# Three norm groups closed with 65 columns, gamma applied by VectorE, and a new order of closings and rounds

## The chip, the cores and the metric

The kernel runs on one core of one Trainium2 chip. The metric is the device time of one execution in microseconds (us), lower is better. TensorE is the matrix engine, VectorE, ScalarE and GpSimd the others that compute; SyncE issues most transfers. A profile names them PE, DVE, ACT, POOL and SP; PEld is TensorE's loading of weights.

## The reference, cut to what matters

```python
def layer0(ego, adj, W_u, diag_u, par_u, W_i, diag_i, par_i, ln_gamma, ln_beta):
    u = par_u[0] * par_u[1] * (diag_u[:, None] * ego[:2048] @ W_u) + ego[:2048]
    i = par_i[0] * par_i[1] * (diag_i[:, None] * ego[2048:] @ W_i) + ego[2048:]
    e = jnp.concatenate([u, i], axis=0)                 # 5120 x 64
    h = adj @ (adj.T @ e)                               # adj 5120 x 5120, float32
    mu, var = jnp.mean(h, -1, keepdims=True), jnp.var(h, -1, keepdims=True)
    return (h - mu) * rsqrt(var + 1e-5) * ln_gamma + ln_beta + ego

x = layernorm(x + layer0(x, adj, ...))
x = layernorm(x + layer1(x, adj, ...))    # graph message passing; zero where no edge survives
```

The second layer's messages are zero if no edge can pass its thresholds. The kernel proves that for its inputs by a bound on the sums of squares of `adj`'s pieces (the maximum below) and takes the long way only if the proof fails. With these inputs it does not take it.

## The kernel before, in words

`adj` passes through the chip once. It is cut into ten blocks of 512 columns, and a block into twenty units of two 128-row tiles. For each unit TensorE multiplies rows of e by it (`multiply_unit`, L1471, which sums adj.T @ e of the block), ScalarE squares and sums it for the maximum, and VectorE transposes it in place. Once a block's sums are complete, its share of h, transposed (64 features by row tiles), is made in rounds (`multiply_round`, L1491), each over some of the forty row tiles: the last block has the rounds LAST (tiles 0 to 11), LAST + 1 (12 to 23), LATE + 1 (24 to 31) and LATE + 2 (32 to 39), and LATE is the last round of the block before, over sixteen tiles (24 to 39). A round's sums lie in four banks of PSUM, and VectorE adds them to `h_sum` (`add_tiles`, L1285), which raises `round_added`. All of LAST + 1 to LATE + 2 use the same banks, so each waits for the addition of the one before.

`h_sum` then is turned to rows and normed in seven groups, `NORM_PARTS`: group k is tiles first to first + nt, sizes 6, 6, 4, 8, 8, 4, 4. To close a group (`close_tiles`, L1506) means one matmul for each tile, with the tile's 128 x 128 piece of `h_sum` as weights and `center` as the moving operand. `center` has 128 columns: 64 give the features less their mean, 64 the same times gamma. `center` is float32, and each such matmul appears in a profile as two passes, two loads and two products. The rest of a group is a chain over engines: ScalarE squares (`square_c`, L1183), VectorE sums (`sum_c`, L1337), GpSimd takes the root (`root_c`, L1107), VectorE scales and adds x (`make_y`, L1357 and L1364, or L1347), ScalarE squares again (`square_y`, L1191), VectorE sums (`sum_y`, L1369), GpSimd takes the second root (`root_y`, L1112), VectorE or ScalarE makes the output (`make_out`), and SyncE stores it.

Each engine works in the order in which its calls are written. `max_found` counts the steps of the maximum: VectorE's partial maximum, TensorE's product that brings it to one row (L1560), VectorE's reduction. Each engine reads the resulting flag once (`edges_may_survive`).

```python
                first, nt = NORM_PARTS[k]
                pe.wait_ge(round_added, added_through(k))
                if k == 1:
                    pe.wait_ge(max_found, 3)
                if k >= 2:
                    pe.wait_ge(t_made, k - 1)
```

Closing 4 is of tiles 24 to 31, so it needs the additions of LATE and LATE + 1; closings 5 and 6 need the two halves of the addition of LATE + 2.

## Time and profile before

| | |
|---|---|
| time, median of 3 runs | 395.99 us (395.52 to 396.37) |
| time of the profiled execution | 397.39 us |
| its span, first to last instruction | 395.5 us |
| TensorE busy | 379.0 us |
| VectorE busy | 316.7 us |
| ScalarE busy | 269.1 us |
| GpSimd busy | 63.8 us |

The span is what the profile shows; starting and ending the program lie around it. Matmuls are pipelined, so a busy TensorE need not be at its peak. Work moves the time only where it lies on the chain that ended last.

### The profile page before, as it was taken

The numbers are of one execution on the slowest core, as the hardware profiler recorded it, in microseconds if no ns is written. First come the engines' busy times: TensorE is split into PE (matmuls) and PEld (weight loads), VectorE is DVE, ScalarE is ACT, GpSimd is POOL, SyncE is SP. The second block draws the span as 40 slices with busy tenths as digits, with TensorE's granted clock in tenths as the row PEclk, the third lists the DMA queues.
The fourth block names the chain that finished last, engine by engine and source line by source line (L and its number), as shares of the span: only waits on it lengthen the run. The fifth ranks groups of instructions, "written<-read, shape, count | busy, mean of one in ns | idle before, by whom it ended". The sixth has DMA issues, their size and how long they took to land.

```text
span 395.5 us, 13309 instructions
## 1 busy us (share of the span) xinstructions
PE 379.0 (96%) x5762; PEld 220.2 (56%) x5762; DVE 316.7 (80%) x305; ACT 269.1 (68%) x519; POOL 63.8 (16%) x122
## 2 busy tenths in 40 slices
PE   8987999999999999999999999999999999999990
PEld 7743655565465546545654664565466456555770
DVE  1699989797697869687976989697698869795674
ACT  3598996994868658597856868685876778511143
POOL 2001101102100300030030003003000300277375
PEclk9999999999999999999999999999999999999996
DMA  8999999995797799579877958996795799400012
GB/s 291 387 388 382 386 386 384 386 352 192 232 380 267 268 320 391 180 275 389 314 263 272 386 195 277 388 351 230 278 386 191 272 392 383 145 3 2 24 35 85
DMA packets 56991, 109.83 MB, mean 278 GB/s; under 512 B 3808, under 2 KB 4576, under 8 KB 56928
## 3 DMA queue, kind: packets, MB, share of 16 engines
q1 hardware_dynamic: 56640, 108.84, 76.3%
q8 instruction: 47, 0.77, 0.8%
q14 instruction: 16, 0.13, 0.1%
q10 hardware_dynamic: 288, 0.09, 0.1%
HBM read 107.60 MB, written 1.31 MB: 275 GB/s over the span
## 4 chain that ended last, share of the span: by engine, by line
PE 84%; DMA 6%; issue 3%; DVE 3%; POOL 1%; ACT 1%; SPq 1%; POOLq 0%; DVEq 0%
PE quad L1491 45%; PE quad L1471 34%; DMA pooled<-in_adj 6%; PE quad L1506 2%; DVE pooled L1265 2%; PE quad L1513 1%; PE quad L1442 1%; ACT scratch L1153 1%; SPq L1033 1%; PE quad L1452 1%; DVE pooled L1285 1%; POOL pooled L1112 1%; POOL col_sum L1084 0%; POOLq L96 0%; POOL pooled L1107 0%
## 5 line engine op out<-in xcount | busy, mean ns | idle before, releaser
L1153 ACT ACTIVATE scratch<-pooled 128x1024 bf16<-128x1024 f32 x200 | 210.1, 1051 | 39.8 <-DMA pooled<-in_adj 38.0
L1265 DVE STREAM_TRANSPOSE pooled<-pooled 128x1024 f32<-128x1024 f32 x200 | 229.7, 1209 | 3.3 <-ACT scratch L1153 3.2
L1471 PE MATMUL quad<-pooled,rows_in 128*64 128x256 f32 x1600 | 180.2, 381 | 4.3 <-DMA pooled<-in_adj 4.3
L1491 PE MATMUL quad<-pooled,col_sum 32*64 32x320 f32 (+4 forms) x3968 | 177.5, 507 | 0.4 <-POOL col_sum L1084 0.2
L1471 PEld LDWEIGHTS quad<-pooled,rows_in 128*64 128x64 f32 x1600 | 111.9, 137 | 74.3 <-issue 13.1
L1491 PEld LDWEIGHTS quad<-pooled,col_sum 32*64 32x64 f32 x3968 | 87.5, 132 | 83.1 <-issue 64.6
L1285 DVE TENSOR_TENSOR pooled<-pooled,quad 128x1280 f32<-128x1280 f32 (+5 forms) x29 | 52.4, 1808 | 43.8 <-PE quad L1491 43.7
L1084 POOL COPY col_sum<-col_half 32x256 f32<-32x256 f32 x80 | 31.6, 394 | 312.1 <-DVE col_half L1274 309.0
L1162 ACT COPY col_sum<-col_half 32x256 f32<-32x256 f32 x80 | 32.2, 402 | 38.0 <-DVE col_half L1274 37.0
L1153 ACT ACTIVATION_READ_ACCUMULATOR scratch<-pooled 128x1 f32 x200 | 37.4, 187 | 0.0
L1183 ACT ACTIVATE pooled<-quad 128x256 f32<-128x256 f32 (+2 forms) x7 | 3.3, 475 | 23.4 <-PE quad L1506 23.4
L1506 PEld LDWEIGHTS quad<-center,pooled 128*128 128x128 f32 x80 | 9.3, 191 | 3.3 <-issue 1.8
L1506 PE MATMUL quad<-center,pooled 128*128 128x128 f32 x80 | 10.3, 281 | 0.9 <-DVE pooled L1285 0.8
L1274 DVE STREAM_TRANSPOSE col_half<-quad 128x256 f32<-128x256 f32 x10 | 4.5, 445 | 7.2 <-PE quad L1471 7.2
L1112 POOL TENSOR_TENSOR pooled<-pooled,minus_half 128x4 f32<-128x4 f32 (+2 forms) x7 | 8.9, 1276 | 6.5 <-DVE pooled L1369 6.4
L1107 POOL TENSOR_TENSOR pooled<-pooled,minus_half 128x4 f32<-128x4 f32 (+2 forms) x7 | 8.9, 1281 | 5.0 <-DVE pooled L1337 4.8
L1191 ACT ACTIVATE pooled<-pooled 128x256 f32<-128x256 f32 (+2 forms) x7 | 3.6, 507 | 9.1 <-DVE pooled L1364 7.2
L1147 ACT COPY pooled<-quad 128x512 f32<-128x512 f32 x5 | 2.9, 585 | 9.7 <-PE quad L1442 9.7
L1283 DVE COPY pooled<-quad 128x1280 f32<-128x1280 f32 (+2 forms) x3 | 5.8, 1936 | 4.1 <-PE quad L1491 4.1
L1238 DVE TENSOR_TENSOR rows_in<-quad,pooled 128x256 f32<-128x256 f32 x10 | 3.7, 410 | 3.6 <-PE quad L1452 3.3
L1102 POOL TENSOR_TENSOR pooled<-pooled,beta_sb 128x512 f32<-128x512 f32 x5 | 6.4, 1276 | 0.4
L1337 DVE TENSOR_REDUCE pooled<-pooled 128x4 f32<-128x260 f32 (+2 forms) x7 | 3.8, 538 | 2.7 <-ACT pooled L1183 2.7
(45 smaller groups left out, 62.8 us busy)
## 6 DMA issues: line engine op xcount, KB each, us to landing
pooled<-in_adj SPq DMA_DIRECT2D x200, 512.0 KB, 9.4
pooled<-in_x SPq DMA_DIRECT2D x5, 256.0 KB, 3.7
pooled<-in_x SPq DMA_DIRECT2D x1, 768.0 KB, 5.3
pooled<-in_x SPq DMA_DIRECT2D x1, 512.0 KB, 3.8
out<-pooled SPq DMA_DIRECT2D x2, 256.0 KB, 2.5
out<-pooled SPq DMA_DIRECT2D x2, 192.0 KB, 2.4
out<-pooled SPq DMA_DIRECT2D x3, 128.0 KB, 2.1
pooled<-in_w_ui ACTq DMA_DIRECT2D x1, 64.0 KB, 3.3
```

Source lines behind the costliest of these rows:

```text
L1084: kept = nc.gpsimd.tensor_copy(spread_to(c, a, h, 1), spread_from(c, h, 1))
L1102: nc.gpsimd.tensor_tensor(xk, xk, beta_sb[:, :].unsqueeze(1).to_broadcast([P, GT, D]), ALU.add).then_inc(x_steps, 1)
L1107: nc.gpsimd.tensor_tensor(rstd[:, norm_tiles(k)], var[:, norm_tiles(k)], minus_half[:, 0:norm_size(k)], ALU.pow).then_inc(rstd_made, 1)
L1112: nc.gpsimd.tensor_tensor(scale[:, norm_tiles(k)], y_var[:, norm_tiles(k)], minus_half[:, 0:norm_size(k)], ALU.pow).then_inc(scale_made, 1)
L1153: nc.scalar.activation(scratch[v % 2][:, :], slots[slot_of(v)], ACT.Square, accum_out=square_sum[:, v:v + 1]).then_inc(unit_scanned, 1)
L1162: kept = act.copy(spread_to(c, a, h, 0), spread_from(c, h, 0))
L1265: nc.vector.transpose(tiles, tiles).then_inc(unit_turned, 1)
L1283: nc.vector.tensor_copy(to, share).then_inc(round_added, 1)
L1285: nc.vector.tensor_tensor(to, to, share, ALU.add).then_inc(round_added, 1)
L1471: mm = pe.matmul(block_bank(c)[half(h), 0:w // 2], rows_in[:, t, :], slots[slot_of(v)][:, at:at + w // 2], start=(t == 0), stop=(t == T - 1))
L1491: mm = pe.matmul(round_banks(g)[a][half(b % 2), 0:w].rearrange("p (t r) -> p t r", r=32), col_sum[c % 2][quadrant(a), b, :], to[quadrant(a ...
L1506: mm = pe.matmul(nat_of(k)[:, i, :], h_sum[:, P * (first + i):P * (first + i) + P], center[:, :], start=True, stop=True)
```

## The change

The first three groups (`NARROW = 3`) are closed with 65 columns of a `center` of 129: 64 centred features and one column with each row's share of gamma's mean. VectorE makes the product with gamma from those, with `gamma_row`, a copy of gamma in all partitions, by two operations a group (`take_c`). The maximum's product moves ahead of the closings, closings 0 and 1 both ahead of round LATE, and 2 and 3 ahead of LATE + 1. The sequences of VectorE, ScalarE and GpSimd are rewritten to suit; groups 0 and 1 exchange the engines that make their output.

```diff
-    BY_ACT, BY_DVE = (1, 2, 3), (0, 4, 5, 6)
+    BY_ACT, BY_DVE = (0, 2, 3), (1, 4, 5, 6)
+    NARROW = 3
-        ln_t = [ln_buffer(D) for _ in range(2)]
+        ln_t = [ln_buffer(D) for _ in range(3)]
-        center = sb("center", [P, 2 * D])
+        center = sb("center", [P, 2 * D + 1])
+        gamma_row = sb("gamma_row", [P, D])
-            return bank[(4 if upper_banks(LAST) else 0) + 3]
+            return bank[(4 if upper_banks(LAST) else 0) + 1][:, CH - P:CH]
...
+                    sp.dma_start(gamma_row[:, :], gamma.rearrange("d o -> (d o)").partition_broadcast(P)).then_inc(norm_in, 16)
...
-                    act.copy(center[:, D:2 * D], bank[3][:, 0:D]).then_inc(center_kept, 1)
+                    act.copy(center[:, 0:D], bank[3][:, 0:D]).then_inc(center_kept, 1)
+                    act.copy(center[:, 2 * D:2 * D + 1], bank[3][:, D:D + 1]).then_inc(center_kept, 1)
...
+                nc.vector.tensor_scalar(center_g[:, D:D + 1], gamma_sb[:, :], 0.5 / D, None, ALU.mult).then_inc(gamma_made, 1)
+                nc.vector.tensor_scalar(gamma_row[:, :], gamma_row[:, :], 0.5, None, ALU.mult).then_inc(gamma_steps, 1)
...
+            def take_c(k):
+
+                nt = norm_size(k)
+                dve.wait_ge(c_squared, k + 1)
+                if k == 0:
+                    dve.wait_ge(gamma_steps, 1)
+                nc.vector.tensor_tensor(ln_t[k][:, 0:nt, :], features_of(k),
+                                        gamma_row[:, :].unsqueeze(1).to_broadcast([P, nt, D]), ALU.mult).then_inc(c_scaled, 1)
+                dve.wait_ge(c_scaled, k + 1)
+                nc.vector.tensor_tensor(ln_t[k][:, 0:nt, :], ln_t[k][:, 0:nt, :],
+                                        nat_of(k)[:, 0:nt, D:D + 1].to_broadcast([P, nt, D]),
+                                        ALU.subtract).then_inc(nat_taken, 1)
...
-                if k == 1:
+                if k >= 2 + NARROW:
+                    pe.wait_ge(t_made, k - 1)
+                elif k >= 2:
+                    pe.wait_ge(nat_taken, k - 1)
+                if k == 2:
                     pe.wait_ge(max_found, 3)
-                if k >= 2:
-                    pe.wait_ge(t_made, k - 1)
+                kinds = slice(D, 2 * D + 1) if k < NARROW else slice(0, 2 * D)
                 for i in range(nt):
-                    mm = pe.matmul(nat_of(k)[:, i, :], h_sum[:, P * (first + i):P * (first + i) + P], center[:, :],
+                    mm = pe.matmul(nat_of(k)[:, i, 0:kinds.stop - kinds.start],
+                                   h_sum[:, P * (first + i):P * (first + i) + P], center[:, kinds],
                                    start=True, stop=True)
...
             multiply_round(LAST)
             multiply_round(LAST + 1)
+            pe.wait_ge(max_found, 1)
+            pe.wait_ge(round_added, added_through(0))
+            pe.matmul(max_bank()[0:1, :], part_max[:, :], ident[:, :], start=True, stop=True).then_inc(max_found, 1)
             close_tiles(0)
-            pe.wait_ge(max_found, 1)
-            pe.matmul(max_bank()[0:1, 0:P], part_max[:, :], ident[:, :], start=True, stop=True).then_inc(max_found, 1)
+            close_tiles(1)
             multiply_round(LATE)
-            close_tiles(1)
             close_tiles(2)
+            close_tiles(3)
             multiply_round(LATE + 1)
-            close_tiles(3)
             close_tiles(4)
             multiply_round(LATE + 2)
```

TensorE before, from round LAST on (L1491 a round, of 64 products; L1506 closings, L1560 the maximum's product):

```order
L1491 MATMUL quad<-pooled,col_sum 64x384 x128
L1506 MATMUL quad<-center,pooled 128x128 x6
L1560 MATMUL quad<-ident,part_max 1x128
L1491 MATMUL quad<-pooled,col_sum 64x512 x64
L1506 MATMUL quad<-center,pooled 128x128 x10
L1491 MATMUL quad<-pooled,col_sum 64x256 x64
L1506 MATMUL quad<-center,pooled 128x128 x16
L1491 MATMUL quad<-pooled,col_sum 64x256 x64
L1506 MATMUL quad<-center,pooled 128x128 x8
```

TensorE with the change, the same stretch (L1526 a round, L1545 closings, L1600 the maximum's product):

```order
L1526 MATMUL quad<-pooled,col_sum 64x384 x128
L1600 MATMUL quad<-ident,part_max 1x128
L1545 MATMUL quad<-center,pooled 128x65 x12
L1526 MATMUL quad<-pooled,col_sum 64x512 x64
L1545 MATMUL quad<-center,pooled 128x65 x4
L1545 MATMUL quad<-center,pooled 128x128 x8
L1526 MATMUL quad<-pooled,col_sum 64x256 x64
L1545 MATMUL quad<-center,pooled 128x128 x8
L1526 MATMUL quad<-pooled,col_sum 64x256 x64
L1545 MATMUL quad<-center,pooled 128x128 x8
```

Twelve tiles in place of six are closed ahead of round LATE, twelve in place of ten ahead of LATE + 1, and eight in place of sixteen ahead of LATE + 2.

VectorE before, between round LAST + 1's addition and LATE's (L1337 sum_c, L1397 and L1399 the maximum and flag, L1357 and L1364 make_y, L1369 sum_y, L1377 make_out, L1285 the addition):

```order
L1337 TENSOR_REDUCE pooled<-pooled 128x6
L1397 TENSOR_REDUCE all_max<-quad 1x1
L1399 TENSOR_SCALAR flag<-all_max 1x1
L1357 TENSOR_TENSOR pooled<-quad,pooled 128x384
L1364 TENSOR_TENSOR pooled<-pooled 128x384
L1369 TENSOR_REDUCE pooled<-pooled 128x6
L459 TENSOR_LOAD flag
L459 ISA x2
L1377 TENSOR_TENSOR pooled<-pooled 128x384
L1285 TENSOR_TENSOR pooled<-pooled,quad 128x4x16x32
```

VectorE with the change, the same stretch up to the read of the flag (L1353 sum_c, L1362 and L1365 take_c, L1432 and L1434 maximum and flag, L1389 and L1396 make_y); the addition follows it:

```order
L1353 TENSOR_REDUCE pooled<-pooled 128x6
L1362 TENSOR_TENSOR pooled<-quad,gamma_row 128x384
L1365 TENSOR_TENSOR pooled<-pooled,quad 128x384
L1353 TENSOR_REDUCE pooled<-pooled 128x6
L1362 TENSOR_TENSOR pooled<-quad,gamma_row 128x384
L1365 TENSOR_TENSOR pooled<-pooled,quad 128x384
L1432 TENSOR_REDUCE all_max<-quad 1x1
L1434 TENSOR_SCALAR flag<-all_max 1x1
L1389 TENSOR_TENSOR pooled<-pooled 128x384
L1396 TENSOR_TENSOR pooled<-pooled 128x384
L1389 TENSOR_TENSOR pooled<-pooled 128x384
L1396 TENSOR_TENSOR pooled<-pooled 128x384
```

Group 1's first half stands there now, with the two operations of take_c for both groups, while group 0's last sum moves behind the addition and its output to ScalarE.

VectorE before, at the last two additions (4x4x32):

```order
L1357 TENSOR_TENSOR pooled<-quad,pooled 128x512
L1285 TENSOR_TENSOR pooled<-pooled,quad 128x4x4x32
L1369 TENSOR_REDUCE pooled<-pooled 128x8
L1285 TENSOR_TENSOR pooled<-pooled,quad 128x4x4x32
L1364 TENSOR_TENSOR pooled<-pooled 128x512
```

VectorE with the change, there (L1401 sum_y, L1409 make_out, L1301 the additions):

```order
L1401 TENSOR_REDUCE pooled<-pooled 128x8
L1409 TENSOR_TENSOR pooled<-pooled 128x384
L1389 TENSOR_TENSOR pooled<-quad,pooled 128x512
L1301 TENSOR_TENSOR pooled<-pooled,quad 128x4x4x32 x2
L1396 TENSOR_TENSOR pooled<-pooled 128x512
```

The sum for group 3 now stands ahead of both additions, and the output of group 1 with it.

## Rows read from the trace of the kernel before

**Rows 1.** The page: engines, GB/s by slice, chain by engine.

```profile
PE 379.0 (96%) x5762; PEld 220.2 (56%) x5762; DVE 316.7 (80%) x305; ACT 269.1 (68%) x519; POOL 63.8 (16%) x122
...
GB/s 291 387 388 382 386 386 384 386 352 192 232 380 267 268 320 391 180 275 389 314 263 272 386 195 277 388 351 230 278 386 191 272 392 383 145 3 2 24 35 85
...
PE 84%; DMA 6%; issue 3%; DVE 3%; POOL 1%; ACT 1%; SPq 1%; POOLq 0%; DVEq 0%
```

**Rows 2.** Timeline, PE, from 359 us: start, length (us), line, count.

```profile
359.72 1.60 PE L1506 MATMUL quad<-center,pooled 128*128 128x128 f32 x12
361.25 0.38 PE L1560 MATMUL quad<-ident,part_max 128*1 128x128 f32 x2
361.79 7.13 PE L1491 MATMUL quad<-pooled,col_sum 32*64 32x512 f32 x128 [0.16 <-DVE pooled L1285]
368.85 2.50 PE L1506 MATMUL quad<-center,pooled 128*128 128x128 f32 x20
371.45 3.71 PE L1491 MATMUL quad<-pooled,col_sum 32*64 32x256 f32 x128
375.09 3.84 PE L1506 MATMUL quad<-center,pooled 128*128 128x128 f32 x32
378.86 3.71 PE L1491 MATMUL quad<-pooled,col_sum 32*64 32x256 f32 x128
383.42 2.36 PE L1506 MATMUL quad<-center,pooled 128*128 128x128 f32 x16 [0.85 <-DVE pooled L1285]
```

**Rows 3.** Timeline, DVE, from 359 us; columns as above.

```profile
359.89 1.75 DVE L1285 TENSOR_TENSOR pooled<-pooled,quad 128x1536 f32<-128x1536 f32 x1 [2.01 <-PE quad L1491]
361.95 0.56 DVE L1337 TENSOR_REDUCE pooled<-pooled 128x6 f32<-128x390 f32 x1 [0.30 <-ACT pooled L1183]
...
364.12 0.56 DVE L1357 TENSOR_TENSOR pooled<-quad,pooled 128x384 f32<-128x384 f32 x1 [1.25 <-POOL pooled L1107]
...
369.01 2.29 DVE L1285 TENSOR_TENSOR pooled<-pooled,quad 128x2048 f32<-128x2048 f32 x1 [0.59 <-PE quad L1491]
...
375.25 1.22 DVE L1285 TENSOR_TENSOR pooled<-pooled,quad 128x1024 f32<-128x1024 f32 x1
...
382.04 0.69 DVE L1357 TENSOR_TENSOR pooled<-quad,pooled 128x512 f32<-128x512 f32 x1 [0.30 <-POOL pooled L1107]
382.68 0.69 DVE L1285 TENSOR_TENSOR pooled<-pooled,quad 128x512 f32<-128x512 f32 x1
...
383.88 0.68 DVE L1285 TENSOR_TENSOR pooled<-pooled,quad 128x512 f32<-128x512 f32 x1
```

**Rows 4.** The chain that ended last, in order of time: start, length, what.

```profile
384.62 1.17 PE quad L1506 x8
...
386.73 1.01 POOL pooled L1107
```

**Rows 5.** Timeline, PEld: loads of weights (rows*columns, then shape).

```profile
9.08 0.97 PEld L1452 LDWEIGHTS quad<-pooled 64*128 64x128 f32 x16 [0.17 <-issue]
...
368.85 2.31 PEld L1506 LDWEIGHTS quad<-center,pooled 128*128 128x128 f32 x20 [0.81 <-issue]
...
383.42 0.97 PEld L1506 LDWEIGHTS quad<-center,pooled 128*128 128x128 f32 x8 [1.30 <-DVE pooled L1285]
```

**Rows 6.** Timeline, ACT and POOL, behind closing 4.

```profile
378.97 0.60 ACT L1183 ACTIVATE pooled<-quad 128x512 f32<-128x512 f32 x1 [1.19 <-PE quad L1506]
...
380.37 1.64 POOL L1107 TENSOR_TENSOR pooled<-pooled,minus_half 128x8 f32<-128x8 f32 x1
```

**Rows 7.** Early: timelines of PE and DVE, PE's waits 40 to 360, issues.

```profile
39.90 4.57 PE L1491 MATMUL quad<-pooled,col_sum 32*64 32x320 f32 x128 [0.16 <-POOL col_sum L1084]
...
56.97 2.02 DVE L1283 COPY pooled<-quad 128x1792 f32<-128x1792 f32 x1 [1.12 <-PE quad L1491]
...
PE quad L1471 <- DMA pooled<-in_adj: 0.7, 3, 0.3
...
beta_sb<-in_beta SPq DMA_DIRECT2D x1, 32.0 KB, 9.7
```

More of the change, by code:

```diff
@@ L66, in adjacency_layers_kernel @@
     NORMS = len(NORM_PARTS)
-    BY_ACT, BY_DVE = (1, 2, 3), (0, 4, 5, 6)
+    BY_ACT, BY_DVE = (0, 2, 3), (1, 4, 5, 6)
+    STORES = (0, 1, 2, 4, 5, 3, 6)
     SHORT = 5
+    NARROW = 3
     BOUND = 0.2
@@ L255, in adjacency_layers_kernel @@
         rstd_made = sem("rstd_made")
+        gamma_steps = sem("gamma_steps")
+        c_scaled = sem("c_scaled")
+        nat_taken = sem("nat_taken")
         t_made = sem("t_made")
@@ L396, in max_bank, with features_of @@
         def max_bank():
-            return bank[(4 if upper_banks(LAST) else 0) + 3]
+            return bank[(4 if upper_banks(LAST) else 0) + 1][:, CH - P:CH]
+        def features_of(k):
+            at = 0 if k < NARROW else D
+            return nat_of(k)[:, 0:norm_size(k), at:at + D]
         def round_sums(g, first, nt):
@@ L1047, in store_made @@
                 store_out(sp, k)
-            for k in (0, 1, 2, 4, 5, 3, 6):
+            for k in STORES:
                 store_made(k)
@@ L1065, in _ @@
                     pool.wait_ge(center_made, 1)
-                nc.gpsimd.affine_select(out=center[:, 0:D], in_=center[:, 0:D], compare_op=ALU.not_equal, fill=1.0,
+                nc.gpsimd.affine_select(out=center[:, D:2 * D], in_=center[:, D:2 * D], compare_op=ALU.not_equal, fill=1.0,
                                         base=-D * h, pattern=[[-1, D]],
@@ L1069, in _ @@
             pool.wait_ge(center_made, 2)
-            nc.gpsimd.tensor_scalar(center[:, 0:D], center[:, 0:D], -1.0 / D, None, ALU.add).then_inc(center_made, 1)
+            nc.gpsimd.tensor_scalar(center[:, D:2 * D], center[:, D:2 * D], -1.0 / D, None, ALU.add).then_inc(center_made, 1)
             pool.wait_ge(ident_made, 1)
@@ L1122, in _ @@
             root_c(0)
+            root_c(1)
+            survives = edges_may_survive(pool)
             root_y(0)
-            survives = edges_may_survive(pool)
-            root_c(1)
             root_c(2)
+            root_c(3)
             root_y(1)
-            root_c(3)
+            root_y(2)
             root_c(4)
-            root_y(2)
             root_y(3)
@@ L1182, in square_c @@
                     act.wait_ge(var_made, k - 1)
[L1183 removed]
+                nc.scalar.activation(c_sq[k % 2][:, 0:norm_size(k), 0:D], features_of(k),
                                      ACT.Square, scale=D ** -0.5).then_inc(c_squared, 1)
@@ L1201, in _ @@
             square_c(0)
+            square_c(1)
+            survives = edges_may_survive(act)
             square_y(0)
-            survives = edges_may_survive(act)
-            square_c(1)
+            square_y(1)
             square_c(2)
-            square_y(1)
+            square_c(3)
+            make_out(0)
             square_y(2)
-            square_c(3)
             square_c(4)
-            make_out(1)
             square_y(3)
@@ L1356, in scale_y @@
                 dve.wait_ge(rstd_made, k + 1)
-                nc.vector.tensor_tensor(ln_t[k % 2][:, 0:nt, :], nat_of(k)[:, 0:nt, D:2 * D],
+                if k < NARROW:
+                    dve.wait_ge(nat_taken, k + 1)
+                source = ln_t[k] if k < NARROW else nat_of(k)
+                nc.vector.tensor_tensor(ln_t[k % 3][:, 0:nt, :], source[:, 0:nt, 0:D],
                                         over_row(rstd[:, tiles], nt), ALU.mult).then_inc(t_made, 1)
@@ L1363, in add_x @@
                 dve.wait_ge(x_steps, 1 + 2 * -(-tiles.stop // GT))
-                nc.vector.tensor_tensor(x_all[:, tiles, :], x_all[:, tiles, :], ln_t[k % 2][:, 0:nt, :],
+                nc.vector.tensor_tensor(x_all[:, tiles, :], x_all[:, tiles, :], ln_t[k % 3][:, 0:nt, :],
                                         ALU.add).then_inc(y_made, 1)
@@ L1395, in _ @@
             sum_c(0)
+            take_c(0)
+            sum_c(1)
+            take_c(1)
             dve.wait_ge(max_found, 2)
-            nc.vector.tensor_reduce(all_max[0:1, :], max_bank()[0:1, 0:P], X, ALU.max).then_inc(max_found, 1)
+            nc.vector.tensor_reduce(all_max[0:1, :], max_bank()[0:1, :], X, ALU.max).then_inc(max_found, 1)
             dve.wait_ge(max_found, 3)
@@ L1400, in _ @@
             make_y(0)
+            make_y(1)
+            survives = edges_may_survive(dve)
+            add_round(LATE)
             sum_y(0)
-            survives = edges_may_survive(dve)
-            make_out(0)
-            add_round(LATE)
-            sum_c(1)
             sum_c(2)
-            make_y(1)
+            sum_c(3)
+            sum_y(1)
+            take_c(2)
+            add_round(LATE + 1)
             make_y(2)
-            add_round(LATE + 1)
-            sum_y(1)
+            make_y(3)
             sum_y(2)
-            sum_c(3)
             sum_c(4)
-            make_y(3)
+            sum_y(3)
+            make_out(1)
             scale_y(4)
             add_tiles(NR - 1, *NORM_PARTS[NORMS - 2])
-            sum_y(3)
             add_tiles(NR - 1, *NORM_PARTS[NORMS - 1])
@@ L1481, in multiply_round @@
                 if g == before_in_banks(NR, False)[0]:
-                    pe.wait_ge(center_kept, 1)
+                    pe.wait_ge(center_kept, 2)
                 same = before_in_banks(g, upper_banks(g))
@@ L1537, in _ @@
             multiply_round(1)
-            pe.wait_ge(gamma_made, 1)
-            pe.matmul(bank[3][:, 0:D], center_t[:, :], center_g[:, :], start=True, stop=True).then_inc(gamma_turned, 1)
+            pe.wait_ge(gamma_made, 2)
+            pe.matmul(bank[3][:, 0:D + 1], center_t[:, :], center_g[:, :], start=True, stop=True).then_inc(gamma_turned, 1)
             for v in range(UNIT_FIRST[1] + 9, UNIT_FIRST[2]):
```

9 lines of the change are left out of this document (4 added, 5 removed).

## The prediction

> **What bounds the kernel now.** I read the page first. TensorE is busy 96% of the span and holds 84% of the chain that ended last [rows 1]. So a change at the end of the program is worth what it does to TensorE's sequence there. The timeline of TensorE from 359 us on shows that sequence: blocks of closings (L1506) and of rounds (L1491), each starting 0.07 us before the printed end of the one ahead, except where a row names a wait [rows 2]. The reader is to see three things in it. At 361.79 the round of sixteen tiles waited 0.16 us for VectorE's addition of round LAST + 1. At 371.45 the next round started 0.15 us after VectorE's addition of 2.29 us had ended at 371.30 [rows 3]: twenty passes of closings just covered it. At 378.86 nothing waited: sixteen tiles were closed after round LATE + 1, and the first eight of them (3.84 us for both, so 1.9) hid the addition of 1.22 us that began at 375.25 and that the second eight need. The chain of waits shows the end: closing 6 at 384.62, then, by way of a square and a sum, GpSimd's last roots from 386.73 on [rows 4]. A closing of one tile is two of the profile's passes.
>
> **What a narrow pass costs.** This decides the case. With 65 columns in place of 128 TensorE streams half as much, but it still loads the same 128 x 128 weights for each tile (a piece of h_sum). The trace has no closing of 65 columns; it has the product at L1452 with 64 moving columns and 128-column weights, sixteen passes that alternate between two halves of the rows, so eight for each half. Their loads fill 0.97 us. The eight loads of a closing of four tiles, which move 128 columns, fill 0.97 us as well [rows 5]. Less the 0.19 us that one load lasts (2.31 us for twenty gives (2.31 - 0.19)/19 = 0.112 us), the period of a load into the same rows is 0.111 to 0.112 us whether 64 or 128 columns follow. I take this as the bound: the load, not the stream, sets a closing's pace, and a narrow pass costs 0.112 us, as a wide one does. The other end: a pass costs what it streams, 65/128 of 0.112, thus 0.057 us. Taken together L1452's sixteen loads come every 0.052 us, but only because those into different halves of the rows overlap, which loads into all 128 rows can't. I stay near the upper end.
>
> The Trainium skill, "TensorE: Matmul & The Clock Gate", section "Back-to-back issue gap", gives an isolated matmul N/2.4 + 2.5 ns, thus 55.8 ns at 128 columns and 29.6 at 65; the trace shows twice the former for a float32 pass, so my estimate by the page is 0.059 us for a narrow pass, and the sum would then be that of the first rival below. The page adds that in a stream the loads count too; L1452 bears that out here.
>
> **The sequence on TensorE, step by step** (times of the profiled run, starts from [rows 2]; p is the narrow pass, 0.112).
> 1. The maximum's product comes first, at 359.72 in place of 361.25. It lasts 0.38 us, 0.31 until the next block: closings start at 360.03. Before, it lay where TensorE would have waited for the addition anyway.
> 2. Closings 0 and 1 are 24 passes. Twenty printed 2.50 us, so 24 make 2.95, and 2.88 until the next block: 362.91. The addition (359.89 + 1.75 = 361.64 [rows 3]) is long done. Before, the round started at 361.79: 1.12 us later.
> 3. Round LATE takes 7.06 us from start to start (361.79 to 368.85): 369.97. Its addition begins 0.16 later and ends at 372.42.
> 4. Closings 2 and 3, 8 narrow and 16 wide passes: 2.88 us, 372.85, past the addition. Before 371.45: 1.40 later.
> 5. Round LATE + 1: 3.64 us (371.45 to 375.09): 376.49. Now closing 4 stands directly behind it and needs h_sum as VectorE's addition leaves it. Before it began 0.16 after 375.09 and took 1.22, and TensorE resumes 0.05 after an addition (that at 382.68 ended 383.37, closing at 383.42). So TensorE idles until 376.49 + 0.16 + 1.22 + 0.05 = 377.92, 1.43 us.
> 6. Closing 4 is 16 passes: 2.50 - 4 x 0.112 = 2.05, 1.98 to the next block: 379.90. Round LATE + 2 follows. Before 378.86: 1.04 later. With starts of loads in place of starts of products I get 1.09.
> 7. The tail. VectorE does the sum for group 3 before round LATE + 2 ends, no longer between the last two additions. Before, the additions began at 382.68 and 383.88, and closing 6 waited for the second, which ended 384.56. Now the second follows 0.60 after the first. Closing 5's eight passes then allow closing 6 at 383.42 + 8 x 0.112 = 384.31 in old times, against 384.62: 0.31 us back. GpSimd's roots for group 3 also move out of the way of the last ones, so from closing 6 on the chain [rows 4] goes as it went.
> Sum: 1.04 to 1.09 less 0.31, that is 0.73 to 0.78 us later.
>
> **The rest of the change.** The scaling by gamma puts six operations on VectorE: four over 128 x 384 at about 0.56 us (as the broadcast product at 364.12, [rows 3]) and two of a third less. Ahead of LATE's addition it has two sums, four such operations, four of make_y and 0.4 us of maximum and flag: 10 x 0.56 + 0.4 = 6.0 us. The first sum starts 0.63 us after closing 0 ended (361.32 to 361.95), now 362.26, so VectorE is ready at 368.3, and the round ends at 369.97: 1.7 us spare. Ahead of LATE + 1's addition, the sum for group 3 can start at 372.92 + 0.63 = 373.5 and 2.1 us of work follow: 375.6 against 376.65. Both additions keep their time, so I cost this at nothing; the cover is those 1.7 and 1.0 us. The way from closing 4 to the addition of tiles 32 to 35 is a second lane beside round LATE + 2: square at 378.97, sum, root at 380.37 with 1.64 us [rows 6], product at 382.04, addition at 382.68 [rows 3]. It moves with closing 4, no further: root_y(2), ahead of it on GpSimd, has its sum about a microsecond earlier. What make_out(0) loses in time on ScalarE only delays a store that nothing waits for.
>
> Early in the program: a third small load on SP's queue beside beta's 32 KB, in a stretch where transfers set TensorE's pace up to about 39 us. Beta's load landed 9.7 us after its issue because of what stood ahead in the queue [rows 7]. Priced by bytes at the 388 GB/s of the page's early slices [rows 1], 32 KB are 0.08 us; round 0 at 39.90 waited for something else, so it costs 0 to 0.1. Two tiny VectorE operations near 46 us (0.15 to 0.3 us each) lie ahead of VectorE's idle time of 1.12 us at 56.97 [rows 7]; one more ScalarE copy of one column has no reader for a long while; from 40 to 360 us TensorE waited only 0.7 us for transfers [rows 7]. I add 0.05 at most. The profiled execution took 397.39 us with a span of 395.5; the median of the runs is 395.99, and I put the difference on that: 395.99 + 0.8 = **396.8 us**. What a measurement here can tell from no change is 0.2%, 0.79 us, so the forecast stands on that line, at 396.78.
>
> **Rivals.**
> - *The stream sets the pace* (p = 0.057). Then closings 0 and 1 end at 361.6, before the addition, and LATE starts at 361.79 as before. Closings 2 and 3 take 2.88 - 8 x 0.055 = 2.44 us, less than the 2.60 from 368.85 to 371.45, so the addition still sets that start. Behind LATE + 1, 1.43 idle and 1.98 for closing 4 stand in place of 3.77: 0.36 us sooner. With 0.31 in the tail it is 0.67 us, 395.3. For it: half the columns. Against it: the loads of L1452. The sum falls by 32 x (0.112 - p), so the sign changes at p = 0.088. Chance 0.10.
> - *VectorE comes late.* If the operations with gamma took twice 0.56 us, LATE's addition would start 4 x 0.56 - 1.7 = 0.5 us late. Closings 2 and 3 give it 2.88 us where it needs 2.60, so 0.2 us reaches LATE + 1. There another 2 x 0.42 us and the 0.5 stand against 1.0 us of margin, so 0.3 us more is added to the idle time: 397.3. For it: no row shows an operation with gamma. Against it: the two margins. Chance 0.10.
> - *In between*: a load of weights follows a shorter stream somewhat sooner, p = 0.100 (0.38 us less), or the tail gives back more: 396.3 to 396.5. Chance 0.12.
> - The forecast, 396.5 to 397.1: 0.68.
>
> **Numbers.** The forecast case lies about the line at 396.78, a little more above it, since both ways of counting and the early costs lead up to 0.83: 0.38 above, 0.30 below. Slower: 0.38 and the late case's 0.10, 0.48. Same: 0.30, 0.12 of the case in between, and half of the stream case, whose 395.3 is just short of 0.2% (395.2): 0.47. Faster: the other half, 0.05. The range, 395.8 to 397.5, leaves out the stream case and the far end of the late one.
>
> **What would show it.** In the changed profile: 24 passes of 128 x 65 in one row of about 2.95 us (1.6 would prove the rival); no wait at the sixteen-tile round; an idle time of about 1.4 us ahead of closing 4, ended by VectorE; closing 6 directly behind closing 5; span near 396.3. A wait ahead of LATE + 1, or one ahead of closing 2 for nat_taken, would make it wrong on the slow side.

## The result, and the profile after

The changed kernel takes 400.38 us (median of 4 runs, 399.14 to 400.85), the kernel before 395.89 in the same measurement. The ratio is 1.0099, with an interval of 1.0083 to 1.0116. The prediction was 396.8, at most 397.5, so it fails. The profiled execution took 400.20 us with a span of 398.0.

The page of the changed kernel: TensorE's busy time, its granted clock by slice, and GB/s by slice.

```profile
PE 379.2 (95%) x5762; PEld 219.2 (55%) x5762; DVE 319.3 (80%) x313; ACT 269.6 (68%) x520; POOL 63.7 (16%) x122
...
PEclk9999899999999999999999999999999999999997
...
GB/s 292 387 387 350 386 387 386 342 390 101 274 391 313 239 301 387 194 272 392 337 250 270 383 197 275 392 355 227 271 386 197 270 392 375 143 3 2 4 54 85
```

TensorE does the same work in the same busy time. Each figure of the last two rows stands for a slice of 10 us. In two places the page differs early on, where the prediction expected nothing: the fourth slice (30 to 40 us) moves 350 GB/s where it moved 382 [rows 1], and the fifth has a clock digit of 8. The timeline of TensorE shows the place. First the kernel before, around units 20 and 21 (L1471); round 0 follows at 39.90 [rows 7]:

```profile
37.33 1.08 PE L1471 MATMUL quad<-pooled,rows_in 128*64 128x256 f32 x8 [0.40 <-DMA pooled<-in_adj]
38.66 1.08 PE L1471 MATMUL quad<-pooled,rows_in 128*64 128x256 f32 x8 [0.25 <-DMA pooled<-in_adj]
...
44.40 5.83 PE L1471 MATMUL quad<-pooled,rows_in 128*64 128x256 f32 x52
```

The same view of the changed kernel:

```profile
39.15 1.08 PE L1506 MATMUL quad<-pooled,rows_in 128*64 128x256 f32 x8 [2.93 <-DMA pooled<-in_adj]
40.49 1.59 PE L1506 MATMUL quad<-pooled,rows_in 128*64 128x256 f32 x8 [0.26 <-DMA pooled<-in_adj]
42.01 5.67 PE L1526 MATMUL quad<-pooled,col_sum 32*64 32x320 f32 x128
47.62 2.59 PE L1506 MATMUL quad<-pooled,rows_in 128*64 128x256 f32 x22
```

TensorE waits 2.93 us for unit 20's part of the adjacency, where it waited 0.40. It is 1.82 us late there, 2.11 at round 0 (42.01 against 39.90), and 3.22 behind round 0 (47.62 against 44.40), because the same 128 products take 5.67 us in place of 4.57. Windows of the changed kernel over that stretch show why (the clock is the third column from the right):

```profile
36.00:39.10 3.10, 0.22 (x3) 0.00 (x0) 3.10 (x5) 1.51 (x5) 0.95 (x3) 1.00 1.00 384
39.10:40.90 1.80, 1.49 (x12) 0.82 (x14) 1.80 (x2) 1.73 (x6) 1.62 (x5) 1.00 1.06 401
40.90:44.40 3.50, 3.50 (x48) 1.59 (x51) 2.77 (x3) 3.48 (x7) 0.58 (x2) 0.51 1.05 387
44.40:47.60 3.20, 3.20 (x104) 1.57 (x88) 0.00 (x0) 3.20 (x9) 0.00 (x0) 1.00 1.07 389
```

After 3.10 us in which TensorE worked for 0.22, the granted clock was 1.00 for another 1.80 us, then 0.51 (the 1.2 GHz level) for 3.50 us, and 1.00 again (2.4 GHz). At the lower level the same products take longer: 0.51 us more in unit 21 (1.59 against 1.08) and 1.10 in round 0.

Of these 3.22 us the two profiles keep 1.82 when the tail begins (361.54 against 359.72). The other 1.4 are the profile of before's own. It waited for transfers again, at two places, where the changed one waited for none from 48 to 360 us:

```profile
122.43 1.08 PE L1471 MATMUL quad<-pooled,rows_in 128*64 128x256 f32 x8 [0.27 <-DMA pooled<-in_adj]
...
157.08 1.08 PE L1471 MATMUL quad<-pooled,rows_in 128*64 128x256 f32 x8 [0.17 <-DMA pooled<-in_adj]
158.45 1.08 PE L1471 MATMUL quad<-pooled,rows_in 128*64 128x256 f32 x8 [0.29 <-DMA pooled<-in_adj]
```

This is also by how much its 397.39 us lay above its median. The trace of rows_load_alone (below) has neither of these waits, and a span of 394.3 us. Then the tail on TensorE, changed kernel (where a row joins passes of two shapes, it prints the first: the second row of x24 is 8 narrow and 16 wide passes):

```profile
361.54 0.38 PE L1600 MATMUL quad<-ident,part_max 128*1 128x128 f32 x2
361.85 2.89 PE L1545 MATMUL quad<-center,pooled 128*128 128x65 f32 x24
364.67 7.12 PE L1526 MATMUL quad<-pooled,col_sum 32*64 32x512 f32 x128
371.72 2.94 PE L1545 MATMUL quad<-center,pooled 128*128 128x65 f32 x24
374.60 3.71 PE L1526 MATMUL quad<-pooled,col_sum 32*64 32x256 f32 x128
379.69 2.05 PE L1545 MATMUL quad<-center,pooled 128*128 128x128 f32 x16 [1.38 <-DVE pooled L1301]
381.67 3.71 PE L1526 MATMUL quad<-pooled,col_sum 32*64 32x256 f32 x128
386.23 2.05 PE L1545 MATMUL quad<-center,pooled 128*128 128x128 f32 x16 [0.85 <-DVE pooled L1301]
```

From the start of the first of these blocks to the end of the last it is 26.74 us; before it was 385.78 - 359.72 = 26.06 [rows 2]. So the tail gives away 0.68 us, where the prediction had 0.73 to 0.78.

**Where the time went.** Early 3.2 us, tail 0.7. A third piece lies outside the span: time less span is 2.19 us on average in the changed kernel's runs, and 1.81 to 1.86 in those of the kernel before, some 0.35 more. The sum, 4.2 to 4.3, stands against a measured 0.0099 x 395.9 = 3.9 (3.3 to 4.6).

### The profile page after: what moved, and what is told of

It reads as the page before. It is cut to its first block, busy times and chain, and to the rows that moved or that the text cites. A ratio compares the mean times of both kernels' runs of the same rounds, so it can differ in the third digit from the quotient of the medians.

```text
span 398.0 us, 13320 instructions
## 1 busy us (share of the span) xinstructions
PE 379.2 (95%) x5762; PEld 219.2 (55%) x5762; DVE 319.3 (80%) x313; ACT 269.6 (68%) x520; POOL 63.7 (16%) x122
## 4 chain that ended last, share of the span: by engine, by line
PE 87%; SPq 7%; DMA 3%; POOL 1%; DVE 1%; issue 0%; POOLq 0%; ACT 0%
PE quad L1526 45%; PE quad L1506 40%; SPq L1046 5%; DMA pooled<-in_adj 3%; PE quad L1545 2%; SPq L1036 1%; POOL pooled L1125 1%; SPq L1031 1%; POOL pooled L1120 0%; DVE pooled L1301 0%; POOLq L98 0%; SPq L1037 0%; DVE pooled L1353 0%; SPq L1038 0%; DVE pooled L1409 0%
## 5 line engine op out<-in xcount | busy, mean ns | idle before, releaser
L1506 PE MATMUL quad<-pooled,rows_in 128*64 128x256 f32 x1600 | 180.1, 382 | 5.4 <-DMA pooled<-in_adj 5.4
L1526 PE MATMUL quad<-pooled,col_sum 32*64 32x320 f32 (+4 forms) x3968 | 178.6, 510 | 0.0
L1506 PEld LDWEIGHTS quad<-pooled,rows_in 128*64 128x64 f32 x1600 | 112.3, 137 | 74.4 <-issue 12.5
L1526 PEld LDWEIGHTS quad<-pooled,col_sum 32*64 32x64 f32 x3968 | 86.3, 133 | 85.0 <-issue 64.1
L1301 DVE TENSOR_TENSOR pooled<-pooled,quad 128x1280 f32<-128x1280 f32 (+5 forms) x29 | 52.3, 1808 | 45.1 <-PE quad L1526 45.1
L1545 PE MATMUL quad<-center,pooled 128*128 128x128 f32 (+1 forms) x80 | 9.9, 279 | 2.2 <-DVE pooled L1301 2.2
L1545 PEld LDWEIGHTS quad<-center,pooled 128*128 128x128 f32 x80 | 9.2, 192 | 4.2 <-DVE pooled L1301 3.1
L1553 PE MATMUL quad<-pooled 128*128 128x256 f32 x10 | 4.6, 650 | 1.2 <-DVE pooled L1238 1.2
```

What stands on the lines that cost most here:

```text
L1301: nc.vector.tensor_tensor(to, to, share, ALU.add).then_inc(round_added, 1)
L1506: mm = pe.matmul(block_bank(c)[half(h), 0:w // 2], rows_in[:, t, :], slots[slot_of(v)][:, at:at + w // 2], start=(t == 0), stop=(t == T - 1))
L1526: mm = pe.matmul(round_banks(g)[a][half(b % 2), 0:w].rearrange("p (t r) -> p t r", r=32), col_sum[c % 2][quadrant(a), b, :], to[quadrant(a ...
L1545: mm = pe.matmul(nat_of(k)[:, i, 0:kinds.stop - kinds.start], h_sum[:, P * (first + i):P * (first + i) + P], center[:, kinds], start=True, ...
```

## The experiments

Each kernel's ratio is to runs of the kernel before on the same chip; 95% intervals in brackets.

### The third small load, by itself and with other contents

gamma_load_alone is the kernel before with the one load added (and VectorE's wait for it):

```
+ sp.dma_start(gamma_row[:, :], gamma.rearrange("d o -> (d o)").partition_broadcast(P)).then_inc(norm_in, 16)
```

> The kernel before, with nothing of the change but the third small load (gamma to all 128 partitions, 256 bytes each) behind beta's, and VectorE waiting for it. Theory A (this load makes some of the transfer engines fall behind, so the parts of the next units land 1 to 2 us later, TensorE idles ahead of unit 20 and its clock drops for a while): the profile shows an idle time of 1.5 us or more ahead of the products at about 37 us, and the time is 1.5 to 4 us over the kernel before. Theory B (the early delay comes from something else in the change, as the reordered tail or the larger center, or is chance): within 0.3 us of the kernel before.

399.71 us, ratio 1.0094 [1.0077, 1.0111], thus 3.7 us: nearly the whole loss. TensorE's timeline:

```profile
39.62 3.33 PE L1473 MATMUL quad<-pooled,rows_in 128*64 128x256 f32 x16 [2.87 <-DMA pooled<-in_adj]
42.88 4.94 PE L1493 MATMUL quad<-pooled,col_sum 32*64 32x320 f32 x128
```

rows_load_alone reads x[0:P, :] instead: the same 32 KB in the same 128 pieces of 256 bytes, but from 128 different places.

> As the run with the gamma load alone, but the load brings 128 different rows of x, 256 bytes each, into the same tile, which nothing reads. Theory A1 (all 128 pieces read the same 256 bytes of HBM, and that is what is slow): no delay, within 0.3 us of the kernel before. Theory A2 (128 short pieces in the queue are what is slow, wherever they read): the same 1.5 to 4 us as with the gamma load.

396.44 us, ratio 1.0002 [0.9991, 1.0013]. It costs nothing that can be measured. So neither the bytes nor the short pieces are the cause; what is left is that one stretch of 256 bytes is read 128 times. gamma_load_twice has the load of gamma's row two times:

> The kernel before with the load of gamma to all partitions added twice, into two tiles, where the run with the gamma load alone has it once (3.3 us of early loss there). If each such load holds back the engines that it meets by about as much again: 6 us or more in all, with the last part of unit 20 landing near 42 us in place of 39.6. If it was one engine's mishap: as with one load, 3 to 4 us.

401.18 us, ratio 1.0122 [1.0104, 1.014], an idle time of 4.59 us ahead of unit 20, whose products start at 41.03. That is 4.8 us in the timed runs and 5.7 in the trace (50.11 behind round 0, against 44.40), short of the 6 expected and more than the 3 to 4 of the other theory. The view of the transfers shows what happens: GB/s from 30 to 42 us, in 40 slices of 0.3 us. The kernel before:

```profile
GB/s 382 382 375 396 396 382 389 375 396 357 342 360 369 375 389 369 410 376 382 376 410 382 369 396 389 375 403 369 403 382 389 375 389 376 396 396 403 369 382 375
```

The changed kernel, with the row above it, the busy share of the DMA engines in tenths (9 is 90% or more):

```profile
DMA  9999999999975866678989999999999999999999
GB/s 382 369 382 369 396 396 382 396 369 367 319 220 219 262 237 237 235 287 322 378 349 349 384 373 379 389 403 416 389 410 396 416 382 389 410 403 369 403 396 369
```

rows_load_alone:

```profile
GB/s 369 376 396 369 382 416 376 389 376 344 350 329 370 362 382 365 380 375 403 369 423 355 382 382 389 389 382 403 376 396 382 382 389 382 382 396 396 355 396 389
```

gamma_load_twice:

```profile
GB/s 376 376 376 382 355 403 382 396 382 351 303 206 151 177 172 179 146 172 173 198 187 225 191 205 230 277 382 362 329 313 361 343 335 362 423 403 423 382 403 396
```

From 33.3 us on, while gamma's row is under way (issued at 27.09, landed at 37.7), everything that the queue carries goes at 220 to 290 GB/s for about two microseconds; with two such loads it is below 230 for four. In the trough the engines are busy only 5 to 8 tenths of a slice; the kernel before has a 9 in each of the 40. So they stand idle between packets.

Unit 20's adjacency, which stands next in the queue, lands late, and not as a whole. The trace records sixteen landings for each transfer. In the changed kernel the first five of unit 20 come at 34.96 to 35.12 us, as in the kernel before (34.94 to 35.10), the other eleven at 35.51 to 39.10, where before they came at 35.12 to 37.28. TensorE needs all sixteen, so the slowest sets its start: from 30 to 42 us 4.29 MB were moved in place of 4.59, which at 383 GB/s is 0.8 us, but the last part was 1.8 us late.

gamma_rows_from_host is the changed kernel, with 128 copies of gamma's row laid out in memory beforehand:

```
- sp.dma_start(gamma_row[:, :], gamma.rearrange("d o -> (d o)").partition_broadcast(P)).then_inc(norm_in, 16)
+ sp.dma_start(gamma_row[:, :], gamma_rows).then_inc(norm_in, 16)
```

> The changed kernel as it is, all three small loads in their place ahead of unit 20, but the third reads 128 copies of gamma that lie one behind the other in HBM (an input laid out so) in place of 128 times the same 256 bytes. Theory A1 (reading the same 256 bytes 128 times holds the engines back): the early loss is gone, the last part of unit 20 lands by 37.5 us, 0.1% to 0.4% over the kernel before. Theory A2 (short pieces, wherever they read): 399 to 401 as the changed kernel.

397.28 us, ratio 1.0021 [1.0006, 1.0037]; the longest early wait is 0.51 us and round 0 starts at 40.23. What is left is what the rest of the change costs. No version with the changed tail has a lower ratio (the intervals of the next ones overlap with it), and it doesn't beat the kernel before.

### Why the load of beta's row did not cost as much

In the kernel before, beta's load copies one row to all partitions as well. beta_row_twice loads beta's row a second time in place of gamma's. beta_from_rows loads gamma's row as gamma_load_alone does, but beta from 128 rows.

```
beta_row_twice:  sp.dma_start(gamma_row[:, :], beta.partition_broadcast(P)).then_inc(norm_in, 16)
beta_from_rows:  sp.dma_start(beta_sb[:, :], beta_rows).then_inc(norm_in, 16)
```

> The kernel before with one more load of 32 KB in the place of the third small load, which copies the row of beta to all 128 partitions, as the load ahead of it already does. Theory A, two loads that each read one stretch of 256 bytes 128 times within a microsecond or two hold the transfers back together: as with gamma's row, about 3.2 us later, ratio 1.008 to 1.010, an idle time of some 2.9 us ahead of unit 20, and a trough near 220 GB/s between 33 and 36 us. Theory B, it is gamma's 256 bytes that are slow to read (the load of single elements ahead of it reads them as well): no loss, within 0.2% of the kernel before, 380 GB/s.

> The kernel before with gamma's row copied to all partitions as in the changed kernel, but beta's load reads 128 rows laid out one behind another, so that only one load of the program reads a stretch of 256 bytes 128 times. Theory A, one such load is nearly free, as beta's is in the kernel before, and the loss comes with the second: within 0.2% of the kernel before and 350 GB/s or more between 33 and 36 us. Theory B, gamma's row is slow by itself: about 3.2 us later, ratio 1.008 to 1.010.

399.3 us, ratio 1.0084 [1.0063, 1.0105], and 396.52 us, ratio 1.0014 [0.9995, 1.0033]. GB/s from 30 to 42 us in beta_row_twice:

```profile
GB/s 423 369 362 369 403 382 369 410 396 345 348 289 278 253 232 218 232 252 274 321 303 357 375 369 362 343 409 410 403 376 416 403 403 376 423 416 362 396 376 376
```

And in beta_from_rows:

```profile
GB/s 430 348 382 369 396 382 376 396 396 359 319 355 335 381 375 388 372 387 362 410 376 376 396 382 403 376 396 382 382 396 376 403 382 389 376 396 389 376 382 382
```

It is not gamma's row: with one copied row the stream stays at 319 GB/s or more, whichever row it is, and the second one directly behind it brings the trough. (Each of these ratios is to a kernel that itself has one copied row; no run is without any.) That is why the trace of before held no warning in beta's load. Why two of them do so, in the memory or in the transfer engines, stays open.

### The loads moved back in time

after_loads_later issues all three small loads behind units 20 and 21 (at v == UNIT_FIRST[1] + 2), before_loads_later does so with the two of the kernel before.

> The changed kernel with its three small loads (gamma, beta, gamma to all partitions) issued behind units 20 and 21 of adj in place of ahead of them. TensorE needs unit 22 only about 4 us after unit 21, since round 0 lies between. Theory A (the loads' place in the queue causes the early loss): the idle time near 37 us is gone and what is left of the change is the tail's 0.7 to 0.8 us, less up to 1 us if the two old loads had cost TensorE time too: 395.5 to 396.8. Theory B (not the loads): 399 to 401 as the changed kernel.

> The kernel before with its two small loads (gamma, beta) issued behind units 20 and 21 in place of ahead of them. If the two loads cost only their bytes: within 0.3 us. If they too make transfer engines fall behind ahead of unit 20: up to 1 us less, 395.0 to 395.6, with the idle times ahead of the products from 31 to 39 us smaller.

398.08 us, ratio 1.0038 [1.0022, 1.0053], and 396.54, ratio 1.0007 [0.9992, 1.0022]. The first missed its 395.5 to 396.8; the second shows no gain from moving the two old loads. TensorE in after_loads_later:

```profile
39.26 4.56 PE L1527 MATMUL quad<-pooled,col_sum 32*64 32x320 f32 x128
43.75 3.83 PE L1507 MATMUL quad<-pooled,rows_in 128*64 128x256 f32 x32
47.85 1.08 PE L1507 MATMUL quad<-pooled,rows_in 128*64 128x256 f32 x8 [0.27 <-DMA pooled<-in_adj]
49.20 1.08 PE L1507 MATMUL quad<-pooled,rows_in 128*64 128x256 f32 x8 [0.27 <-DMA pooled<-in_adj]
```

Round 0 now starts 0.64 us sooner than before, at the full clock, and the delay comes back behind it as three waits of 0.26 to 0.27 us. They are short, and the clock doesn't fall. The next round starts at 51.56, 0.97 us later than before (50.59): moved back, the loads cost 1.0 us in place of 3.2, not nothing, and this is what the expectation missed.

### The tail without the early load

after_row_at_end is the changed kernel with gamma's row loaded near the end, behind the reloads of x, and halved by VectorE there. Nothing else is moved.

> The changed kernel with the load of gamma to all partitions (and its halving on VectorE) moved to the end of the program, behind the last load of x, where no transfer of adj is left; gamma and beta stay where they were. Theory A (the early loss is that load, the rest is the tail): the tail's 0.7 to 0.8 us are left, 0.1% to 0.3% over the kernel before, with no idle time over 1 us ahead of unit 20. Theory B (something else of the change costs in the main part too): 0.5% or more.

397.52 us, ratio 1.0035 [1.0022, 1.0048], between the two theories' bounds. No early stall; the tail shows the same blocks of 24 passes in 2.89 and 2.94 us and 1.39 us idle. The rest of the change costs 0.9 to 1.9 us; its two known parts, 0.7 in the tail and 0.35 outside the span, make 1.0. The kernels below have this base.

closings_128_columns gives the first three groups' products 128 columns, 63 of which are zeros, at the same place in the same order (`center` is widened to suit):

```
- kinds = slice(D, 2 * D + 1) if k < NARROW else slice(0, 2 * D)
+ kinds = slice(D, 3 * D) if k < NARROW else slice(0, 2 * D)
```

> As the run with the row at the end, but the first three groups are closed with 128 moving columns again, 65 as now and 63 of zeros, in the same order. Prediction's theory (the load of 128 columns of weights sets a pass, 0.112 us at 65 and at 128 columns): the row of 24 passes is 2.9 to 2.95 us as with 65, and the time is the same within 0.1 us. Rival (the stream sets it): 24 wide passes would be 1.3 us longer than narrow ones.

397.29 us, ratio 1.003 [1.0019, 1.0041]. Its first closings on TensorE:

```profile
358.62 2.94 PE L1546 MATMUL quad<-center,pooled 128*128 128x128 f32 x24
```

Taking the columns back to 128 adds 0.05 us to the printed length, which is the last pass, and doesn't make the kernel measurably slower (397.29 against 397.52). closings_16_columns and closings_32_columns go the other way; each leaves out the other columns of these groups' products, and each was run once.

> As the run with the row at the end, but the first three groups are closed with 16 moving columns only; the other 49 are left out, so the norms read what is not computed. Prediction's theory: still 0.11 us a pass, 2.7 to 2.9 us for 24 passes, since each still loads 128 columns. If a pass gets shorter with the stream once the load is no longer alone at work: well under 2.5 us.

> As the run with the row at the end, but the first three groups are closed with 32 moving columns; the other 33 are left out. With 16 columns the granted clock fell during the closings and round LATE took 10.0 us in place of 7.1. [...] A pass stays at 0.11 us while the clock is high, since the load sets it.

399.8 and 399.31 us: slower. TensorE in closings_16_columns:

```profile
358.20 3.23 PE L1546 MATMUL quad<-center,pooled 128*128 128x16 f32 x24
361.36 10.05 PE L1527 MATMUL quad<-pooled,col_sum 32*64 32x512 f32 x128
371.34 2.94 PE L1546 MATMUL quad<-center,pooled 128*128 128x16 f32 x24
```

Its windows:

```profile
358.00:361.00 3.00, 3.00 (x25) 2.80 (x24) 2.41 (x3) 0.49 (x1) 2.25 (x2) 0.92 0.02 5
361.00:367.00 6.00, 6.00 (x59) 2.28 (x66) 4.95 (x11) 1.54 (x3) 2.69 (x2) 0.50 0.00 1
367.00:371.00 4.00, 4.00 (x80) 1.24 (x64) 0.00 (x0) 0.00 (x0) 0.00 (x0) 0.96 0.02 4
```

And in closings_32_columns TensorE, then windows:

```profile
359.36 2.87 PE L1546 MATMUL quad<-center,pooled 128*128 128x32 f32 x24
362.16 8.82 PE L1527 MATMUL quad<-pooled,col_sum 32*64 32x512 f32 x128
```

```profile
362.10:362.70 0.60, 0.60 (x18) 0.31 (x25) 0.57 (x2) 0.43 (x1) 0.48 (x1) 1.00 0.00 0
362.80:366.10 3.30, 3.30 (x47) 1.17 (x36) 3.19 (x9) 0.00 (x0) 2.11 (x2) 0.50 0.00 0
```

Two things are to be read. A block of 24 passes at the full clock takes 2.87 to 2.94 us whether 32, 65 or 128 columns move. With 16 the block printed 3.23, not the 2.7 to 2.9 expected, because the clock fell within it, at 360.5; the twenty passes up to there start 0.112 us apart, as with more columns, and those behind it 0.214. What all of them share is the load of 128 columns of weights, so it sets the pace. And in or just behind such a block of 16 or 32 columns the granted clock fell to the lower level with no idle time at all on TensorE, so that the round of sixteen tiles took 10.05 and 8.82 us in place of 7.12.

order_undone has the old order in the tail on all engines, with the 65 columns and the scaling by gamma on VectorE kept. TensorE's order, in words:

```
  for closings: max product first; close_tiles(0); round LATE; close_tiles(1), (2); round LATE + 1; close_tiles(3), (4)
```

> From the run with the row at the end (65 columns, gamma by VectorE, its load late), the order of the tail is put back: closing 0 alone ahead of round LATE (behind the maximum's product), 1 and 2 ahead of LATE + 1, 3 and 4 behind it, and the sequences of the other engines as before, with take_c between. Theory (the tail's loss is the order: 24 passes ahead of LATE and an addition behind which nothing is left to close): the idle time of 1.4 us ahead of closing 4 is gone and the time is that of the kernel before, within 0.2%. Rival (the loss is gamma on VectorE or the narrow closings): still 0.2% or more over it. From TensorE's side nothing is gained by 65 columns, so not faster than before either.

397.2 us, ratio 1.0028 [1.0011, 1.0045]; this missed its expectation of at most 0.2%. Its timelines, TensorE first and then VectorE and GpSimd:

```profile
374.24 3.84 PE L1546 MATMUL quad<-center,pooled 128*128 128x128 f32 x32
378.00 3.71 PE L1527 MATMUL quad<-pooled,col_sum 32*64 32x256 f32 x128
382.86 2.36 PE L1546 MATMUL quad<-center,pooled 128*128 128x128 f32 x16 [1.15 <-DVE pooled L1300]
```

```profile
377.38 0.69 DVE L1352 TENSOR_REDUCE pooled<-pooled 128x8 f32<-128x520 f32 x1
...
380.00 0.69 DVE L1388 TENSOR_TENSOR pooled<-quad,pooled 128x512 f32<-128x512 f32 x1 [0.56 <-POOL pooled L1120]
```

```profile
378.25 3.24 POOL L1120 TENSOR_TENSOR pooled<-pooled,minus_half 128x8 f32<-128x8 f32 x2
```

The idle time ahead of closing 4 is gone, as expected. But with the operations for gamma ahead of it VectorE comes to the sum for group 3 late: 3.14 us behind the start of the block of 32 (377.38 - 374.24), where before it was 2.72 (377.81 - 375.09). GpSimd's roots for groups 3 and 4 then follow each other without a gap (x2, 3.24 us), make_y(3) starts at 380.00, and closing 5 waits 1.15 us in place of 0.85 [rows 2]. In the traces the tail is 0.30 us longer than before; the new order has 0.68. By the timed runs alone, 1.0028 and 1.0035, the two orders can't be told apart.

### The time outside the span

Every kernel with the changed code has 2.16 to 2.22 us outside the span; the kernel before and those with only a load more have 1.80 to 1.87. The change declares three semaphores. Three kernels are the one before with three or twelve more that nothing uses, and with three that memsets of one column on VectorE count up.

```
+ spare = [sem(f"spare{k}") for k in range(3)]
...
+ for k in range(3):
+     nc.vector.memset(spare_at[:, k:k + 1], 0.0).then_inc(spare[k], 1)
```

> The kernel before with three more semaphores allocated, as the change allocates three (gamma_steps, c_scaled, nat_taken), and not used. In every run so far the time outside the span was 1.81 to 1.89 us for kernels with the old set and 2.16 to 2.22 with the new. Theory S (the number allocated sets it): 2.2 us outside the span. Theory C (it is the code or the use, not the allocation): 1.8 to 1.9.

> As the run with three more semaphores, but twelve. Theory S: if each costs 0.12 us, 3.2 us outside the span; if it is a step, 2.2. Theory C and U: 1.8 to 1.9.

> As the run with three more semaphores, and VectorE raises each once, with three small memsets ahead of its last transposition. Theory U (semaphores that a program uses have to be cleared, so use sets it): 2.2 us outside the span here and 1.8 to 1.9 in the run that only allocates them. Theory C: 1.8 to 1.9 in both.

The ratios are 0.9985 [0.9968, 1.0001], 1.0001 [0.9983, 1.0019] and 0.9996 [0.9979, 1.0012]: none makes a difference that can be measured. Outside the span they have 1.86, 1.82 and 2.21 us. So the 0.35 us come with three semaphores in use, or with the memsets that use them, and not with declaring them. Whether they lengthen the whole is not shown: the spans of that kernel were shorter by 0.3 us in the median.

## Why the prediction was wrong

**The step that failed** is the costing of the early load: "Priced by bytes at the 388 GB/s of the page's early slices [rows 1], 32 KB are 0.08 us; round 0 at 39.90 waited for something else, so it costs 0 to 0.1." It measured 3.2 us in the traces, and 3.7 (3.0 to 4.4) in the timed runs of gamma_load_alone. The price took all bytes as alike, and rows_load_alone agrees with this for bytes from 128 places (0.1 us, at most 0.5). For a second row copied to all partitions it is wrong by a factor of forty: some of the sixteen parts of unit 20 fell up to 1.8 us behind, TensorE waited 2.93 us for the last, and its clock fell. The row from which the price could have been bounded didn't exist in the trace: beta's load is of the same kind, but alone it brings no trough (342 GB/s at the least). What could have been seen is that nothing had any margin there: TensorE was waiting for transfers for units 19 to 21, and no upper end above 0.1 us was set for an operation that the trace showed only once. Also, "round 0 waited for something else" was no cover: its wait of 0.16 us for GpSimd only hides delays of the adjacency up to that size. And a long enough wait costs more than itself, since 1.1 of the 3.2 us are round 0 at the lower clock.

**What was right.**
- *A narrow pass costs what a wide one does.* 24 passes printed 2.89 us (2.95 expected; the rival's 1.6 is refuted), and 128 columns at the same place took 2.94. The Trainium skill, "TensorE: Matmul & The Clock Gate", section "LDWEIGHTS (loading the stationary operand)", puts a load at its columns over 1.2, in ns, which makes an estimate of 107 ns for 128 columns; the pace of 0.112 us at 16 to 128 moving columns agrees with it.
- *Closings 2 and 3 behind LATE* took 2.88 us to the next block (2.88 expected), LATE + 1 had 3.71 printed as before, and closing 4 waited 1.38 us for VectorE (1.43 expected). It then took 2.05 (2.05).
- *The tail's 0.31 us back*: closing 6 stands directly behind closing 5, in one row of x16 that printed 2.05 in place of 2.36. The tail as a whole came to 0.68 (0.73 to 0.78 expected).
- *VectorE's cover* held. In the changed kernel's timeline it waits 2.19 us ahead of LATE's addition and 1.13 us ahead of that of LATE + 1 (1.7 and 1.0 expected), and the six operations for gamma cost what others of their shape do (0.55 and 0.42 us):

```profile
366.03 0.55 DVE L1362 TENSOR_TENSOR pooled<-quad,gamma_row 128x384 f32<-128x384 f32 x1
...
371.90 2.29 DVE L1301 TENSOR_TENSOR pooled<-pooled,quad 128x2048 f32<-128x2048 f32 x1 [2.19 <-PE quad L1526]
...
378.41 1.22 DVE L1301 TENSOR_TENSOR pooled<-pooled,quad 128x1024 f32<-128x1024 f32 x1 [1.13 <-PE quad L1526]
```

One row was read loosely, without effect on the sum: the addition was not "just covered" by twenty passes at 371.45, since by the spacing of the other blocks the round could have started at 371.28.

**What was missing besides**: 0.35 us outside the span, of which the trace's timelines show nothing. Without the early load the changed kernel has ratios of 1.0021 and 1.0035, which at 395.99 are 396.8 and 397.4 us, inside the predicted range; the load alone carried it out. That the first of them is the very forecast is in part luck, as the 0.35 was not in the sum.

**Why the change doesn't pay.** What it halves, the columns that TensorE streams, was not what set the pace, so no time comes back there. What it adds is a load that holds up the adjacency, a closing that waits for VectorE with nothing ahead to hide it, and work on VectorE that the old order feels too (0.30 us in the trace of order_undone).

## What to carry to other kernels

Price a transfer by how it reads, not only by its bytes: a second load that copies one short row to all partitions, close behind a first, took the whole stream from about 385 to 220 GB/s for two microseconds. Put it where no transfer is on the path, or read from distinct rows. Before a product is made narrower, compare its pace with that of loads of its weights: with a new 128 x 128 load for each product, fewer moving columns brought nothing here, and with 16 and 32 (one run each) the clock went down. Where transfers set an engine's pace, give every added transfer an upper end, however small it is.

## What was not expected of the hardware

- With one load of 128 copies of 256 bytes the stream showed no trough, and which row is copied made no difference (1.0014). A second one cost 3.3 to 3.7 us (1.0084 and 1.0094), two more 4.8 (1.0122). The same number of short pieces from distinct places cost nothing measurable (1.0002). The Trainium skill, "DMA: Bandwidth & Descriptors", section "Specifications", asks for 512 bytes or more in a transfer for the full rate; by that the short pieces would be the cause, and rows_load_alone, with the same pieces at 329 to 423 GB/s, shows that here they weren't.
- A load is as late as the last of its sixteen parts: with 0.8 us worth of bytes missing, unit 20 was 1.8 us late, while five of its parts came on time.
- A wait of 2.93 us on TensorE was followed, 1.8 us after its end, by 3.5 us at half the clock, which cost 1.1 us in the next round. The waits of 2.87, 3.01 and 4.59 us in gamma_load_alone, beta_row_twice and gamma_load_twice were followed by a fall too (0.55, 0.63 and 0.50 from 41 to 44 us); three waits of 0.27 us in a row were not.
- The clock also fell in or just behind a block of 24 passes with 16 or 32 moving columns and no idle time, and cost 2.9 and 1.7 us in the round behind it (10.05 and 8.82 against 7.12). With 65 columns it stayed up.
- Three semaphores in use went with 0.38 us more outside the span, declared alone with none.
